# Twelve chunks summed ahead in DRAM, three gathers per two steps, weights loaded inside the steps

## Time and profile before

| | |
|---|---|
| median of 3 runs | 2157.56 us (2151.57 to 2160.16) |
| profiled execution | 2155.56 us |
| its span, first to last instruction | 2153.8 us |
| busy share | PE 87%, DVE 85%, ACT 87%, POOL 90% |
| mean granted TensorE clock | 0.957 |
| moved by DMA | 447.92 MB, 208 GB/s |
| queue q1 (SP) | 302.61 MB, 42.9% of 16 engines' span |
| queue q0 (POOL) | 142.61 MB, 34.2% |

### The profile page before, as it was taken

The page is one execution under the profiler, slowest core; times in us unless marked ns, Lnnn a source line. Parts: engine busy times, 40 slices in busy tenths (PEclk is TensorE's granted clock), DMA queues, the critical chain, the costliest instruction groups (busy, mean ns, idle before and its releaser), DMA issues.

```text
span 2153.8 us, 42420 instructions
## 1 busy us (share of the span) xinstructions
PE 1873.0 (87%) x11917; PEld 1286.6 (60%) x11917; DVE 1822.8 (85%) x4612; ACT 1882.0 (87%) x5020; POOL 1939.2 (90%) x2068
## 2 busy tenths in 40 slices
PE   6999999999999999999999999999999987636991
PEld 6866666666666666666666666666666643213570
DVE  4689999999999898989899999999999899624670
ACT  6899999999999999999999999999999987743420
POOL 5799999999999999999999999999999999961387
PEclk9999999999999999999999999999999998765995
DMA  5498888887888888888788888888788676694963
GB/s 188 157 262 222 228 223 206 226 229 216 218 218 235 224 227 210 224 231 222 215 216 231 229 224 220 212 229 227 213 222 223 178 182 162 165 263 124 282 104 32
DMA packets 111068, 447.92 MB, mean 208 GB/s; under 512 B 10575, under 2 KB 52404, under 8 KB 61684
## 3 DMA queue, kind: packets, MB, share of 16 engines
q1 hardware_dynamic: 81140, 302.61, 42.9%
q0 software_dynamic: 29696, 142.61, 34.2%
HBM read 306.78 MB, written 138.41 MB: 207 GB/s over the span
## 4 chain that ended last, share of the span: by engine, by line
ACT 38%; POOL 21%; issue 17%; PE 16%; DVE 5%; ACTq 1%; DMA 1%; POOLq 0%; SPq 0%; DVEq 0%
ACT U L553 16%; POOL U L430 8%; POOL U L435 7%; ACT zT L516 6%; ACT UT L510 6%; PE G L747 4%; ACT LTS L580 3%; ACT LTS L525 3%; PE T L729 3%; PE O L680 2%; POOL zn L451 2%; POOL out_dram L490 2%; PE T L736 1%; ACT zn L574 1%; POOL U L442 1%
## 5 line engine op out<-in xcount | busy, mean ns | idle before, releaser
L553 ACT ACTIVATE U<-xa,nA,rA 128x128 f32<-128x128 f32 x1948 | 803.7, 483 | 2.1 <-issue 1.3
L747 PEld LDWEIGHTS G<-UT 128*128 128x128 f32 x4096 | 536.8, 192 | 226.5 <-issue 225.3
L430 POOL TENSOR_TENSOR U<-U,bet 128x512 f32<-128x512 f32 x512 | 651.4, 1272 | 2.2
L435 POOL TENSOR_TENSOR U<-U,rO 128x512 f32<-128x512 f32 x512 | 532.2, 1040 | 20.3 <-ACT rO L533 19.3
L747 PE MATMUL G<-UT 128*128 128x128 f32 x4096 | 542.0, 275 | 0.0
L680 PE MATMUL O<-U,MT 128*128 128x512 f32 x1024 | 529.5, 599 | 3.0 <-DVE U L938 3.0
L451 POOL TENSOR_TENSOR zn<-U,rZ 128x512 f32<-128x512 f32 x414 | 446.6, 1079 | 11.0 <-ACT rZ L564 10.3
L936 DVE BATCH_NORM_STATS2 stO<-O 128x6 f32<-128x256 f32 x1024 | 386.8, 423 | 50.2 <-PE O L680 49.5
L729 PE MATMUL T<-ident,U 128*128 128x128 f32 x2048 | 324.3, 281 | 119.1 <-ACT UT L510 108.6
L729 PEld LDWEIGHTS T<-ident,U 128*128 128x128 f32 x2048 | 224.6, 142 | 318.1 <-issue 314.1
L954 DVE BATCH_NORM_STATS2 stA<-xa 128x6 f32<-128x256 f32 x1024 | 386.8, 426 | 31.8 <-DMA xa<-in_x 28.5
(11 more groups left out here) (151 smaller groups left out, 1655.0 us busy)
## 6 DMA issues: line engine op xcount, KB each, us to landing
xa<-in_x SPq DMA_DIRECT2D x128, 1024.0 KB, 6.3
U<-in_x POOLq DMA_DIRECT2D x128, 1024.0 KB, 10.8
out_dram<-U SPq DMA_DIRECT2D x128, 1024.0 KB, 8.6
U<-in_L_ffn_weight SPq DMA_DIRECT2D x112, 256.0 KB
LTS<-in_L_ffn_weight SPq DMA_DIRECT2D x16, 256.0 KB
xa<-out_dram,UT POOLq DMA_INDIRECT x64
out_dram<-U,UT POOLq DMA_INDIRECT x64
zT<-in_L_ffn_weight SPq DMA_DIRECT2D x1, 128.0 KB
```

Of the source, the lines that this page charges most:

```text
L430: gp.tensor_tensor(rows(a, i), rows(a, i), bet_b, ALU.add).then_inc(S["gb"], 1)
L435: gp.tensor_tensor(rows(a, i), rows(a, i), rO[:, i // 2 % 2, i % 2 * TI:(i % 2 + 1) * TI].unsqueeze(2).to_broadcast([P, TI, W]), ALU.mult) ...
L553: last = sc.activation(utile(a, i, j), xa[:, k % XR, h * W:(h + 1) * W], ACT.Identity, scale=rA[:, k % 2, h:h + 1], bias=nA[:, k % 2, h:h ...
L747: last = te.matmul(G[:, 0:P], v, v, start=(i == 0 and j == 0), stop=(i == NI - 1 and j == TI - 1))
```

## The change

- The last 12 chunks (from X_BETA = 116, items 464 to 511, so steps 527 to 574 of BETA) get no beta addition on POOL. Instead, their place in out is filled in DRAM before: at step 96 SP writes beta, repeated, to 4 chunks (4 transfers of 1 MiB in pieces of a row of 512 bytes); at steps 128 and 160 it copies these 4 MiB to the next two groups of 4 chunks; at steps 192, 224 and 256 POOL adds x to each group with an accumulating transfer of 4 MiB, DRAM to DRAM. ACC of those chunks then reads out instead of x, and waits for Y instead of BETA.
- Gathers start at step 540, three in two steps, 52 in the steps (images 0 to 12) and 12 behind them. The spread and places of images 0 to 12 come at steps 536 and 538, those of 13 and 14 at 577 and 579. All zn go to ACT from step 540 on, two items more than before (467 and 471).
- Weights of 20 experts are issued by SP inside the steps, two experts at each fourth step from 528 to 564, each pair once the zn of the chunk that held its place is made.

```diff
-PARTS = ((545, 0, 14), (576, 14, 15))
-S_GATH = 549
+PARTS = ((536, 0, 13), (577, 13, 15))
+S_GATH = 540
...
+X_BETA = 14 * NK + NK // 2
+S_PRE, S_SUM = (96, 128, 160), (192, 224, 256)
...
+        def quad(v, m):
+
+            b, k = divmod(X_BETA + 4 * m, NK)
+            return v[:, b:b + 1, k * CW:(k + 4) * CW]
...
                 for t in range(NI):
+                    for m, step in enumerate(S_PRE):
+                        if once(b, t, step):
+                            if m == 0:
+
+                                c, k = divmod(X_BETA, NK)
+                                for d in range(4):
+                                    sp.dma_start(out_v[:, c, (k + d) * CW:(k + d + 1) * CW].rearrange("c (h w) -> c h w", w=W),
+                                                 bet[:, :].unsqueeze(1).to_broadcast([P, TC, W])).then_inc(s_pre, 16)
+                            else:
+                                sp.wait_ge(s_pre, 16 * 4)
+                                sp.dma_start(quad(out_v, m), quad(out_v, 0)).then_inc(s_pre, 16)
                     if r := item(b, t, L_LOAD, IC):
...
-            bodies(sp, body)
+                    if (r := item(b, t, L_ZN + IC, IC)) and r[0][0] >= NB - 2:
+
+                        a, k = r
+                        e = a[0] % 2 * EQN + 2 * k
+                        if e < EQN + 4:
+                            wait_zn(sp, a, IC * k + IC - 1)
+                            sp.wait_ge(s_store[a[0] % 2 * NK + k], 16 * (NB // 2))
+                            weights(e)
+                            weights(e + 1)
...
-            wait_zn(sp, (NB - 2, None), NI - 1)
-            for k in range(NK):
-                sp.wait_ge(s_store[k], 16 * (NB // 2))
-            for e in range(EQN):
-                weights(e)
-            wait_zn(sp, (NB - 1, None), NI - 1)
-            for k in range(NK):
-                sp.wait_ge(s_store[NK + k], 16 * (NB // 2))
-            for e in range(EQN, EQN + 4):
-                weights(e)
+            bodies(sp, body)
...
-                    if r := item(b, t, L_BETA):
+                    for m, step in enumerate(S_SUM):
+                        if once(b, t, step):
+                            pool.wait_ge(s_pre, 16 * 6)
+                            gp.dma_start(quad(out_v, m), quad(x_v, m), accum_op=ALU.add, max_dma_last_dim=4 * CW).then_inc(s_sum, 16)
+                    if (r := item(b, t, L_BETA)) and r[0][0] * NI + r[1] < X_BETA * IC:
...
-                        pool.wait_ge(S["gb"], cnt(a, NI, IC * k + IC))
+                        n = a[0] * NK + k
+                        if n < X_BETA:
+                            pool.wait_ge(S["gb"], cnt(a, NI, IC * k + IC))
+                        else:
+                            pool.wait_ge(S["y"], cnt(a, NI, IC * k + IC))
+                            pool.wait_ge(s_sum, 16 * ((n - X_BETA) // 4 + 1))
                         bv = val(a)
                         gp.dma_start(U[:, a[0] % 2, k:k + 1, :],
-                                     x_v[:, bass.ds(bv, 1), k * CW:(k + 1) * CW],
+                                     (x_v if n < X_BETA else out_v)[:, bass.ds(bv, 1), k * CW:(k + 1) * CW],
...
-                    if 0 <= g < Q * (NB - 2):
+                    for g in range(max(0, 3 * g // 2), min(3 * (g + 1) // 2, Q * (NB - 3))):
...
-                        gather(*divmod(g, NB - 2))
+                        gather(*divmod(g, NB - 3))
...
-            for n in (NB - 2, NB - 1):
-                pool.wait_ge(R_["idx"], n - NB + 4)
+            for n in range(NB - 3, NB):
+                if n == NB - 1:
+
+                    pool.wait_ge(S["trz"], NB * NI)
...
+                pool.wait_ge(R_["idx"], 3 if n == NB - 1 else 2)
```

More of the change, by code:

```diff
@@ L202, in program @@
         s_store = [sem(f"s_store{i}") for i in range(2 * NK)]
-        s_setup_dve = sem("s_setup_dve")
+        s_setup_dve = sem("s_setup_dve"); s_pre = sem("s_pre"); s_sum = sem("s_sum")
         names = ("a_bn a_ln a_rstd a_nmu u_ready tru ut_ready gram g_copied a1 a1s att att_s "
@@ L460, in body @@
                                 pool.wait_ge(s_store[k], 16 * (NB // 2 - 1))
-                        gather(*divmod(g, NB - 2))
+                        gather(*divmod(g, NB - 3))
             bodies(pool, body)
[L467 to L471, removed]
-            for n in (NB - 2, NB - 1):
-                pool.wait_ge(R_["idx"], n - NB + 4)
+            for n in range(NB - 3, NB):
+                if n == NB - 1:
+                    pool.wait_ge(S["trz"], NB * NI)
+                    gp.memset(before, 1.0).then_inc(s_prep, 1)
+                    pool.wait_ge(s_prep, 2)
+                    gp.affine_select(out=before, in_=before, compare_op=ALU.is_gt, fill=0.0,
+                                     base=0, pattern=[[-1, P]], channel_multiplier=1).then_inc(s_prep, 1)
+                pool.wait_ge(R_["idx"], 3 if n == NB - 1 else 2)
                 for k in range(NK):
-                    pool.wait_ge(s_store[n % 2 * NK + k], 16 * (NB // 2))
+                    pool.wait_ge(s_store[n % 2 * NK + k], 16 * (n // 2 + 1))
                 for q in range(Q):
```

## The result

| | before | after |
|---|---|---|
| median | 2157.55 us | 2184.97 us (2177.09 to 2187.84, 4 runs) |
| profiled execution | 2155.56 us | 2182.91 us |
| its span | 2153.8 us | 2181.1 us |
| mean granted TensorE clock | 0.957 | 0.951 |

The ratio is 1.0113, with a 95% interval of 1.0088 to 1.0139: slower, by 27 us or 1.1%. The forecast was 20 us slower, in a range of 2132 to 2212 us.

The account below looks back on a forecast made before the run. ACT's pace was taken to bound the steady part, DVE and POOL the stretch after, POOL alone the late gathers. From 2155.56 us, minus 28 at the end, plus 48 early: 2176 us; range 2132 to 2212, forecast's own 2168 to 2195.

Parts of the forecast that it names:

- 16.2 us late: Step 192: accumulate queued behind the 4 MiB sum lands at 577.5, where DVE reads its target at 561.33; 4.8 us absorbed.
- The estimate by alternation at packet borders: Step 192: 32 KB packets let SP's 8 KB packets through singly; DVE meets the load first, over 20 us after issue.
- The row's price: Copies at steps 128, 160: 4 MiB priced at 12.9 us from the nearest profile row, which has one end in DRAM.
- The estimate by the Trainium skill: Copies at steps 128, 160: 207 GB/s per direction makes a copy 20 us, the total some 8 us later.
- the quarter that I put on top of the row: Copies at steps 128, 160: 16.1 us taken instead of 12.9, so 5.5 us stay each, 11 together.
- For steps 549 to 573 ... 16 us: POOL without beta, with denser gathers: 0.65 us less a step over 25 steps, 16 us won.
- 1.5 lost: Steps 540 to 548, which had no gathers before: POOL's 3.07 us a step is 0.17 more than 2.9.
- If the y of step 573 is not some 13 us nearer to that of step 527, POOL was not the bound: Sign to check in the profile after, on whether POOL bounds the late steps 527 to 573.
- The gap: ACT's pauses before the last zT copies, 12.66 and 5.55 us: moving weights into steps 528 to 564 saves 15 us.
- the landing of the last accumulate then meets no burst: End of the chain: with ten MiB of weights issued in steps 528 to 564, ACT's pauses go, 15 us saved.
- the weights don't take the gap away: Rival, end: the pause comes between the steps or does not hang on weights; costs back 15, 2191 us; chance 0.12.
- The rival of swallowed sums: Steady stretch: pipeline absorbs the sums, early cost under 17 us, kernel faster at 2148 or 2133 us; chance 0.21.

Follow-up runs that it names:

- run in pieces: Changed kernel with the DRAM work as twelve 1 MiB fills on SP, no copies, and twelve 1 MiB sums, one per 32 steps: 2132.05 us, ratio 0.9867.
- run with pieces only: Kernel before plus the spread 1 MiB fills and sums, without the 48 beta additions, its gathers and weights as they were: 2146.38 us, ratio 0.9943.
- weights-only run: Kernel before with only the weights of 20 experts moved inside the steps: 2152.89 us, ratio 0.9983.

## Why the prediction was right, and where not

**The sums: right in mechanism and size.** "16.2 us late" was measured as 15.94, 16.32 and 15.66, "34 us for three" as 34.9; of DVE's three waits 13.0 us were absorbed, 4.3 each for 4.8. The queue's arithmetic held in detail: after the sum's landing the next accumulate took 4.8 us (5.2 charged). The runs without sums and in pieces exclude the other readings. The estimate by alternation at packet borders had DVE meet the load first, "over 20 us after its issue". The load took 11.9 us and DVE waited 0.47 us for it. What failed there is its premise, packets of 32 KB for the sum: they had 8 KB. The rule itself (the Trainium skill, DMA: Bandwidth & Descriptors, section Queues, rings and completion order) the trace agrees with, as far as equal numbers of packets from both queues show it: 387 and 393 beside the sum, 105 and 113 beside the copy.

**The copies: 14.1 us for 11.** The row's price was right: 6.4 + 5.2 + 12.9 = 24.5 us to the landing, 23.7 measured. The estimate by the Trainium skill (DMA: Bandwidth & Descriptors, section Latency and other measured facts), 20 us for the copy alone, would have given 31.6, and the measurement decides against it here. The 207 GB/s of the Trainium skill belong to a row pitch of 512 KiB, and the rows here lie 64 KiB apart: what fails is carrying the figure over, and no run here tests the figure itself. The measurement speaks against the quarter that I put on top of the row as well. Two other steps failed. I had DVE meet the load of x in the copy's own queue late. That load did land late, 18.7 us after its issue, but DVE met the accumulate in the other queue first; I had counted its 5.2 us as something that the copy waits for, and not seen that it ends no sooner than the copy. And I let 4.8 us be absorbed: DVE waited 7.09 and 6.85, and 6.6 and 7.5 stayed. Why nothing was absorbed there is not settled.

**The fill: 5.4 us for 3.** The failed step is that I priced the bytes and not SP's issuing. Four transfers in pieces of 512 B, one behind the other, held SP for 20.11 us, the load behind them came late by that, and DVE stood 11.94 us. It is their standing together: alone, one such transfer took SP 0.43 us in the run in pieces. What SP waits for in the 20 us the trace doesn't say.

**POOL at the end.** "For steps 549 to 573 ... 16 us": 91.2 - 75.0 = 16.2, and 3.13 us a step for "every 3.1 us". Late landing of the last accumulate: 11.95 us for 8.2, 3.7 where 4 were taken off. From step 522 to 540: 2.7 for 1.5. The mis-sized term is steps 540 to 548: "1.5 lost" were 8.4. I had set POOL's time for them, but DVE bounds there, 35.34 of 36 us busy: it makes the row numbers and merges the top 8 of an image in this stretch, and POOL stood 3.46 and 4.75 us for it, 8.2 together. In the kernel before DVE was as full, but made the row numbers only at the end of these steps (1788 to 1793 us), and POOL, busy 24.42 of the 27 us, had no such wait. In the run with pieces only, whose row numbers and gathers come at the old steps, Y loses 0.8 us from step 540 to 549, so the 8.4 belong to the earlier gathers with their row numbers, and not to beta's absence. From step 527 to 573 Y comes 9.2 us nearer. "If the y of step 573 is not some 13 us nearer to that of step 527, POOL was not the bound" thus speaks against POOL; that holds for steps 540 to 548, where DVE bounds, and not for 549 to 573, where POOL's pace came as forecast.

**The gap: right in size, wrong in cause.** From the last Y to the last zT 16.6 us were won. With the 3.7 lost at the accumulate and the 1.3 of the beta won there, the pauses gave some 19, where 15 were taken. But the step "the landing of the last accumulate then meets no burst" failed. Moving the weights alone leaves the pauses; leaving the weights behind brings none back. They come with long rows of gathers back to back, and go with them. The rival "the weights don't take the gap away" was right in its "does not hang on the weights at all", and wrong that the 15 us would come back, since the denser gathers of this same change shorten the row from 30 to 8.

Together 55 - 28 = 27 for 48 - 28 = 20: the early terms were 7 short, and at the end 7 lost in steps 540 to 548 stand against some 4 more from the pauses and smaller parts. That the end gave just the 28 of the forecast is luck to that extent. The rival of swallowed sums falls with the measured waits; with pieces it comes true.

## What to carry to other kernels

A transfer that nobody waits for still delays the steady ones behind it: compare its length with the margin of the next transfer in the queue, and cut it into pieces shorter than that, each in a place of its own. Twelve MiB cost 35 us in three places and under 1 us in twelve; four pieces in one place cost as much as the whole. Look also at what an issuing engine needs for several transfers in small pieces one behind the other, and not only at the bytes; and don't issue a long row of indirect gathers from POOL beside short exchanges between PE, ACT and DVE, but spread them over steps in which POOL has time.

## What the runs showed of the hardware

- Long rows of indirect gathers 1.25 us apart on POOL come with pauses in the exchange between PE and ACT: with 30 in a row ACT lost 15.14 and 15.08 us in the pieces-only run, 7.26 and 8.31 in the weights-only run, at DMA shares of 1.00 and 0.21. Beside a row of 16 ACT lost 11.50 us, beside rows of 8 and 11 nothing that the traces show. The profile names no releaser ("issue", "remote"). What the stopped engines wait for stays open: shown is only that the pauses come and go with such rows.
- A copy DRAM to DRAM in SP's queue delays a transfer that POOL issues 1.9 us later in its own queue: 21.7 us to landing for 11.0. While both queues have work, the engines take nearly as many packets from one as from the other (105 and 113, 387 and 393), so large packets in one queue slow the other one.
- An accumulate DRAM to DRAM costs what one into SBUF costs: by the packets in the trace 0.63 us of an engine for 8 KB beside 0.64, and the accumulate behind the sum landed 4.8 us after it for 5.2 charged. Its packets had 8 KB though it was written with rows of 32 KB; a plain copy so written moved in packets of 32 KB.
- Four transfers with pieces of 512 B, issued one behind the other, took SP 20.11 us to issue; such transfers one at a time took 0.43 each, and a load of the same size 0.33.
